# Five edits to a fused state-space, linear-attention and expert kernel: squares summed in pairs on VectorE, query decay spread by DMA, decay remainders on VectorE, step sizes two stages sooner, the second load of x into the first norm's buffer

## Time and profile before

| | us |
|---|---|
| median of 3 runs | 2577.02 (2574.51 to 2595.25) |
| the profiled execution | 2582.14, its span 2580.3 |
| opening of attention to opening of attention, one round | 1372.43 to 1495.92: 123.5 |
| PE busy in the span | 2221.5 (86%) |
| DVE busy | 1871.7 (73%) |
| ACT busy | 1469.4 (57%) |
| POOL busy | 813.6 (32%) |

### The profile page before, as it was taken

One profiled execution on the slowest core, in us unless ns is written; L12 is line 12 of the kernel. 1 busy time (PEld: TensorE's weight loads), 2 busy tenths in 40 slices (PEclk: granted clock), 3 DMA queues, 4 the chain that ended last, 5 costly groups with the idle time before them and its releaser, 6 DMA issues. The chain is left out here.

```text
span 2580.3 us, 53740 instructions
## 1 busy us (share of the span) xinstructions
PE 2221.5 (86%) x16824; PEld 1658.7 (64%) x16825; DVE 1871.7 (73%) x3521; ACT 1469.4 (57%) x3336; POOL 813.6 (32%) x1092
## 2 busy tenths in 40 slices
PE   3489898999889898989898989899989939999990
PEld 1247565666657565757575757575757739999990
DVE  2796869685968686777777786869685437777778
ACT  2276666665666566666666666667665603333334
POOL 0112414141414141414142323233242323334346
PEclk9599999998999899999999999999989969999995
DMA  4531414141423232323132223324140032222216
GB/s 121 119 90 43 103 38 99 41 97 40 97 58 84 53 83 68 79 61 87 51 87 66 71 66 71 86 52 98 39 107 5 10 132 58 59 57 56 60 46 195
DMA packets 144122, 189.19 MB, mean 73 GB/s; under 512 B 16984, under 2 KB 92768, under 8 KB 143552
## 3 DMA queue, kind: packets, MB, share of 16 engines
q1 hardware_dynamic: 121680, 118.72, 15.9%
q0 software_dynamic: 22272, 67.92, 12.4%
HBM read 109.77 MB, written 27.56 MB: 53 GB/s over the span
## 5 line engine op out<-in xcount | busy, mean ns | idle before, releaser
L1407 DVE TENSOR_TENSOR_SCAN hs<-decay,push 128x512 f32<-128x512 f32 x256 | 351.2, 1393 | 26.0 <-ACT decay L1069 20.5
L1156 ACT ACTIVATE S<-banks,fall_tok 128x128 f32<-128x128 f32 x1024 | 278.5, 385 | 28.4 <-PE banks L786 28.4
L978 PE MATMUL banks<-rowsT,w_here 128*128 128x128 f32 x2176 | 269.3, 277 | 7.3 <-DVE w_here L1731 7.3
L1512 DVE SCALAR_TENSOR_TENSOR oT<-tog,banks 128x512 f32<-128x512 f32 x128 | 87.6, 684 | 243.5 <-ACT sq L1123 243.3
L978 PEld LDWEIGHTS banks<-rowsT,w_here 128*128 128x128 f32 x2176 | 255.9, 193 | 10.7 <-issue 9.8
L1505 DVE TENSOR_TENSOR S<-banks,S 128x512 f32<-128x512 f32 x256 | 170.8, 687 | 104.2 <-PE banks L798 98.0
L1810 POOL DMA_DIRECT2D y<-ch x96 | 88.7, 924 | 498.8 <-DVE ch L1415 397.3
L1908 POOL TENSOR_TENSOR qd<-q,qd 128x512 f32<-128x512 f32 x96 | 134.1, 1397 | 292.0 <-ACT qd L1141 292.0
L1951 POOL DMA_INDIRECT results_scratch<-rows_out,result_to x136 | 132.3, 973 | 241.1 <-ACT rows_out L1285 234.4
L1274 ACT ACTIVATE tanh_h<-banks 128x512 f32<-128x512 f32 x136 | 81.3, 598 | 203.7 <-PE banks L978 203.7
L1069 ACT ACTIVATE decay<-delta,a_neg 128x512 f32<-128x512 f32 x256 | 171.9, 729 | 17.7 <-DVE hs L1407 17.1
(11 more groups left out here) (221 smaller groups left out, 5361.2 us busy)
## 6 DMA issues: line engine op xcount, KB each, us to landing
y<-ch POOLq DMA_DIRECT2D x96, 512.0 KB, 6.2
b_all<-bc_scratch SPq DMA_DIRECT2D x128, 256.0 KB, 5.5
c_all<-bc_scratch SPq DMA_DIRECT2D x128, 256.0 KB, 3.6
rows_in<-rows_scratch SPq DMA_DIRECT2D x136, 66.0 KB
both<-results_scratch SPq DMA_DIRECT2D x32, 256.0 KB, 3.5
w<-w_dram SPq DMA_DIRECT2D x3, 2048.0 KB, 8.9
x_tok<-x_dram SPq DMA_DIRECT2D x16, 256.0 KB, 3.3
x_again<-x_dram SPq DMA_DIRECT2D x16, 256.0 KB, 2.9
```

The costliest lines, as they stand in the source:

```text
L978: mm = pe.matmul(bank_h[:, u % 2, n, here], w_here[:, u % 2, n, here], x, start=True, stop=True)
L1156: ins = nc.scalar.activation(S[:, g, here], bank[:, here], ACT.Exp, bias=fall_tok[:, head:head + 1])
L1407: nc.vector.tensor_tensor_scan(hs[:, h, :], decay[:, n % 2, h, :], push[:, h, :], 0.0, ALU.mult, ALU.add).then_inc(s_scan, 1)
```

## The change

Five edits; both kernels compute the same function.

1. `sq_less`: DVE adds the two halves of `sq` (128x256) after each gating, and PE sums 4 blocks per chunk in place of 8. `project_out` waits for it.
2. The heads are stored even ones first. ACT takes exp(-fall) of 16 rows once per round into `fall_exp` (it shares the buffer of `sp_ln`), SP stores it to DRAM (two DMAs) and reads it back spread over 64 partitions each, twice per stage for stages 2 to 7, into `q_fall` with two slots. The uses `e`, their 24 matmuls per round and the 6 exponentials on ACT go; `chunk_fall` becomes a copy. POOL's multiplication reads `q_fall`. In a stage POOL now does `decay_queries` and the scatters ahead of `sum_state`. SP issues spreads 4 to 7 behind the last state's spread, each waiting for the multiplication two stages before it.
3. `fall_less` goes from POOL to DVE, in units 3 and 4.
4. `dt` goes to stage 4, DVE's part to stage 5; z goes to stage 6 and waits with its tanh for the step sizes.
5. The second load of x goes into `x1`, which is free only when the next sub-layer's sum is taken ("ffn", stage 6; before: "mix", stage 4). `take` copies to a buffer `x2_kept`, and the wait for the scatters moves to DVE's first `residual`, in stage 3.

```diff
 def front_uses(h):
 
     c, f = divmod(h, 2)
-    uses = [f"e{f}_{c}"] if c else []
-    uses += [f"v{f}_{c}"]
+    uses = [f"v{f}_{c}"]
...
-FRONT = {"xT": 0, "u0": 1, "u1": 2, "xdbl": 3, "z0": 5, "z1": 5, "dt0": 6, "dt1": 6}
-SIZES_STAGE, BC_STAGE, TAKE_STAGE, X3_AFTER = 7, 3, 2, 3
+FRONT = {"xT": 0, "u0": 1, "u1": 2, "xdbl": 3, "dt0": 4, "dt1": 4, "z0": 6, "z1": 6}
+SIZES_STAGE, BC_STAGE, TAKE_STAGE, X3_AFTER = 5, 3, 2, 4
+FALLS_AFTER = 3
+SPREAD_AFTER = {4: (2, 3), 7: (4, 5, 6, 7)}
...
             def body(i, j, n):
                 if i is not None:
                     if not first(i):
-                        drained(sp, ring, i - 1, "mix")
-                    sp.dma_start(x_again[:], x_dram[bass.ds(i, 1)].rearrange("b p c d -> (b p) c d")
+                        drained(sp, ring, i - 1, "ffn")
+                    sp.dma_start(x1[:], x_dram[bass.ds(i, 1)].rearrange("b p c d -> (b p) c d")
                                  ).then_inc(s_x_again, 16)
...
-                for m in range(STATES if i is not None else 0):
-                    spread_bc(m, i)
-                    if m == X3_AFTER and j is not None and not first(j):
-                        store_x3(j - 1)
-                if i is None and j is not None:
-                    store_x3(j - 1)
+                for m in range(STATES):
+                    if i is not None:
+                        spread_bc(m, i)
+                    if j is not None:
+                        if m == FALLS_AFTER:
+                            store_falls(j)
+                        if m == X3_AFTER and not first(j):
+                            store_x3(j - 1)
+                        for h in SPREAD_AFTER.get(m, ()):
+                            spread_falls(h, j)
...
+            def store_falls(j):
+
+                sp.wait_ge(s_fall_exp, at(j, 1, 1))
+                for odd in range(2):
+                    sp.dma_start(fall_dram[bass.ds(j, 1), odd].rearrange("b c h n -> (b h) c n"),
+                                 fall_exp[odd * PAIRS:(odd + 1) * PAIRS, :].rearrange("h (c n) -> h c n", n=P)
+                                 ).then_inc(s_fall_stored, 16)
+
+            def spread_falls(h, j):
+
+                c, f = divmod(h, 2)
+                if h == 2:
+                    sp.wait_ge(s_fall_stored, at(j, 32, 32))
+                if h >= 4:
+                    sp.wait_ge(s_qd, at(j, STAGES - 2, h - 3))
+                for odd in range(2):
+                    sp.dma_start(q_fall[odd * DH:(odd + 1) * DH, f, :],
+                                 fall_dram[bass.ds(j, 1), odd, c, 4 * f:4 * f + 4, :].rearrange(
+                                     "b h n -> b (h n)").broadcast_to([DH, 4 * P])).then_inc(s_q_fall[f], 16)
...
-                if c:
-                    bank, full = fill(ring, f"e{f}_{c}", j)
-                    for t in range(4):
-                        mm = pe.matmul(bank[:, t * P:(t + 1) * P], nselpair[:, 4 * f + t, :],
-                                       fall_parts[:, here], start=True, stop=True)
-                    mm.then_inc(full, 1)
...
                 pe.wait_ge(s_og, at(j, STAGES, 2 * c + 2))
+                pe.wait_ge(s_sq_less, at(j, STAGES, 2 * c + 2))
                 bank, full = fill(ring, f"wo_{c}", it)
                 for t in range(PAIRS):
                     pe.matmul(bank[:, 0:P], oT[:, t, :], w_o[:, t, :], start=(t == 0), stop=(t == PAIRS - 1))
-                for t in range(PAIRS):
-                    mm = pe.matmul(bank[:, P:P + 1], sq[:, t // 4, t % 4 * P:(t % 4 + 1) * P], ones[:, 0:1],
-                                   start=(t == 0), stop=(t == PAIRS - 1))
+                for t in range(PAIRS // 2):
+                    mm = pe.matmul(bank[:, P:P + 1], sq_less[:, t // 2, t % 2 * P:(t % 2 + 1) * P], ones[:, 0:1],
+                                   start=(t == 0), stop=(t == PAIRS // 2 - 1))
                 mm.then_inc(full, 1)
...
@@ -1041,7 +1066,7 @@
 
             def gate_input(h, n):
                 bank = full(ring, f"z{h}", n)
-                act.wait_ge(s_xc, at(n, HALVES, h + 1))
+                act.wait_ge(s_delta, at(n, HALVES, HALVES))
...
@@ -1053,7 +1078,8 @@
                 for h in range(HALVES):
                     nc.scalar.activation(delta[:, h, :], full(ring, f"dt{h}", n), ACT.Identity,
                                          bias=b_dt[:, h:h + 1]).then_inc(ring.free_sem(f"dt{h}"), 1)
-                drained(act, ring, n, "dt0", "dt1", "z0", "z1")
+                drained(act, ring, n, "dt0", "dt1")
+                act.wait_ge(s_xc, at(n, HALVES, HALVES))
                 nc.scalar.activation(th[:], delta[:], ACT.Abs).then_inc(s_sp, 1)
...
@@ -1093,6 +1120,7 @@
                 if n == 0:
                     act.wait_ge(s_fall, at(j, TILES, TILES))
                     nc.scalar.copy(fall_parts[:], fall[:]).then_inc(s_fsplit, 1)
+                    nc.scalar.activation(fall_exp[0:HEADS, :], fall[0:HEADS, :], ACT.Exp, scale=-1.0).then_inc(s_fall_exp, 1)
...
@@ -1134,11 +1163,10 @@
                 if h == 0:
                     after(act, s_O, at(j, STAGES, 0))
                 if c:
-                    falls = full(ring, f"e{f}_{c}", j).rearrange("p (t n) -> p t n", n=P)
+                    act.wait_ge(s_q_fall[f], at(j, 32 * (TILES - 1), 32 * c))
                     if c > 1:
                         act.wait_ge(s_decst, at(j, STAGES - 4, h - 3))
-                    nc.scalar.activation(chunk_fall[:, pairs], falls[:, :, P - 1], ACT.Exp).then_inc(s_kept, 1)
-                    nc.scalar.activation(qd[:, pairs, :], falls, ACT.Exp).then_inc(ring.free_sem(f"e{f}_{c}"), 1)
+                    nc.scalar.copy(chunk_fall[:, pairs], q_fall[:, f, P - 1::P]).then_inc(s_kept, 1)
...
@@ -1172,11 +1200,8 @@
             def take(j):
 
                 act.wait_ge(s_x2, at(j, TILES, TILES))
-                if not first(j):
-                    act.wait_ge(s_x3_stored, at(j, 16, 0))
-                    act.wait_ge(ring.full_sem("x3T"), ring.full_at("x3T", j))
-                    act.wait_ge(s_scattered, at(j, 16 * 2 * TILES, 0))
-                nc.scalar.copy(x3[:], x2_new[:]).then_inc(s_x2_taken, 1)
+                after(act, s_residual, at(j, TILES, 0))
+                nc.scalar.copy(x2_kept[:], x2_new[:]).then_inc(s_x2_taken, 1)
...
@@ -1199,11 +1224,11 @@
                             convolved(half, n)
                     if h == BC_STAGE:
                         parameters(n)
+                    if h == FRONT["dt1"]:
+                        steps(n)
                     for half in range(HALVES):
                         if h == FRONT[f"z{half}"]:
                             gate_input(half, n)
-                    if h == FRONT["dt1"]:
-                        steps(n)
...
+                after(dve, s_fall_exp, at(j, 1, 0))
...
+            def fall_less(n, j):
+
+                dve.wait_ge(s_fsplit, at(j, 5, 2 * n + 1))
+                if n == 0:
+                    nc.vector.tensor_tensor(fall_rest[:], fall[:], fall_parts[:], ALU.subtract).then_inc(s_fsplit, 1)
+                else:
+
+                    nc.vector.tensor_tensor(fall_rest[:], fall_rest[:], fall_parts[:], ALU.subtract).then_inc(s_fsplit, 1)
...
+                nc.vector.tensor_tensor(sq_less[:, f, :], sq[:, f, 0:2 * P], sq[:, f, 2 * P:4 * P], ALU.add
+                                        ).then_inc(s_sq_less, 1)
 
...
@@ -1587,11 +1628,11 @@
                     if h == NORM2_STAGE:
                         normalize(x2_new, s_rstd1, s_x2, i)
                 if n is not None:
+                    if h == SIZES_STAGE:
+                        step_sizes(n)
                     for half in range(HALVES):
                         if h == FRONT[f"z{half}"]:
                             gate_input(half, n)
-                    if h == SIZES_STAGE:
-                        step_sizes(n)
...
+                        if u in FALL_PARTS[:2]:
+                            fall_less(FALL_PARTS.index(u), j)
...
                 pairs = slice(4 * f, 4 * f + 4)
                 if c == 1:
                     drained(pool, ring, j, *(f"q{p}" for p in range(4 * f, 4 * f + 4)))
-                drained(pool, ring, j, f"e{f}_{c}")
-                nc.gpsimd.tensor_tensor(qd[:, pairs, :], q[:, pairs, c * P:(c + 1) * P], qd[:, pairs, :], ALU.mult
-                                        ).then_inc(s_qd, 1)
+                pool.wait_ge(s_q_fall[f], at(j, 32 * (TILES - 1), 32 * c))
+                pool.wait_ge(s_kept, at(j, STAGES - 2, h - 1))
+                after(pool, s_O, at(j, STAGES, h - 1))
+                nc.gpsimd.tensor_tensor(qd[:, pairs, :], q[:, pairs, c * P:(c + 1) * P],
+                                        q_fall[:, f, :].rearrange("p (t n) -> p t n", n=P), ALU.mult).then_inc(s_qd, 1)
...
             def stage(h, i, j):
                 m = STATE_IN_STAGE.get(h) if i is not None else None
-                if m is not None and m <= SUMS:
-                    sum_state(m, i)
```

(15 more changed lines are left out.)

38 lines of the change are left out of this document (16 added, 22 removed).

## The result

| | before | after |
|---|---|---|
| median, same chip | 2586.14 (2574.51 to 2611.83, 4 runs) | 2472.99 (2471.17 to 2474.75, 4 runs) |
| ratio, 95% interval | | 0.9576 (0.9539 to 0.9613) |
| span of the profiled run | 2580.3 | 2472.9 |
| granted clock over the span | 0.935 | 0.951 |
| opening to opening, mean of 12 rounds of the loop | 124.45 | 116.92 |

The kernel is 4.2% faster by the ratio. By these medians that is 113 us, and 104 against the 2577.0 from which the forecast started; forecast were 51. A round lost 7.5, not 3.1. (In this part a round is the mean of the same 12, worked out from PE's list: openings at 368.65 to 1862.09 before, 356.81 to 1759.82 after.)

A forecast was written before the change was run, and what follows sets the result against it. DVE was taken to set the pace from unit 2 to stage 2, PE from stage 3 on and in units 0 to 2. Terms summed to -3.1 per round, -51 together, giving 2526 from the median 2577.0; range 2490 to 2568.

The forecast's parts named there:

- 3.16 at the jump back of the loop: PE's wait at the loop's end, listed among the few places where PE stands still; no term was given for it.
- At the start of a round DVE is ready earlier, but its next work waits for the RMS scale, so nothing comes of it.: Start of a round: moving the step sizes earlier gains nothing there.
- Squares: PE's four one-column sums per round, halved: -0.85 for chunk 3 in unit 0, -2.55 for stages 2, 4 and 6.
- Pair products: PE's six sets of four matmuls dropped, stages 1 to 6: 0 in stages 1 and 2, -0.92 for the other four.
- Decay remainders: Moved from POOL to DVE beside the scans of states 2 and 3: -1.15 per round, bounds -2.6 to +1.4.
- Sum of squares on DVE: DVE's new additions, eight per round at 0.415; the first two, in DVE's regime, cost +0.8.
- Bank in stage 4: PE's second mask waits for DVE's state addition, delayed by collisions with POOL's products: +1.1 per round, 0 to 2.3.
- x1T copy: Stage 6: ACT copies the turned x1 behind its mask exponentials and PE waits: +0.5 per round, 0 to 1.5.
- Spreads, loads, scatters: The spreads' and next round's loads' DMAs stay covered, and the scatters have landed by DVE's stage 3: 0.
- slower rival: States' sum lands late and DVE stands 5.4 in stage 3: +2.3 per round, 2607; chance 0.07.
- faster rival: POOL's products miss DVE's new sums, so stage 4's wait is 0: -4.2 per round, 2509; chance 0.2.

The follow-up runs named there:

- e9: Changed kernel with 56 more PE instructions (satisfied waits) and the residual's load of x back in its own buffer behind stage 4's sum: 2507.09, ratio 0.9688.
- e7: Changed kernel with 56 more PE instructions per round, satisfied waits spread over places where PE stands anyway: 2536.53, ratio 0.9842 to the kernel before.
- e2: Changed kernel with edit 4 undone, so step sizes late again: 2508.37, ratio 0.9705 to the kernel before.
- e6: Kernel before with edit 4 alone, the earlier step sizes: 2580.48, ratio 1.000.
- e8: Changed kernel with edit 3 undone, POOL computing the decay remainders again: 2489.65, ratio 0.9651 to the kernel before.
- e3: Kernel before with edit 1 alone, squares halved on DVE and 4 sums per chunk on PE: 2549.04, ratio 0.984.
- e10: Changed kernel with DVE's halved sum of squares moved behind the state addition, in stage 7 behind x_new's normalisation: 2470.70, ratio 0.9546 to the kernel before.
- e11: Changed kernel with 24 more PE instructions per round, satisfied waits: 2473.61, ratio 0.9551 to the kernel before.
- e1: Changed kernel with 112 more PE instructions per round, satisfied waits ahead of two keys and the choice of experts: 2588.38, ratio 1.000 to the kernel before.

## Why the prediction was wrong, point by point

The direction was right, the size was half of what was measured. Compared by stretches of a round (predicted, measured): opening to x3's transpose -0.85, -2.12; from there to the scores of stage 3 -0.35, +0.72; the rest -1.87, -6.14.

- **The step that failed** is in the first paragraph: "3.16 at the jump back of the loop" was put down as a stall of fixed size and never priced. It was a fetch that hung on the length of PE's body. e9 is nearly the changed kernel with such a jump left in it (wait 2.78 by issue) and stands at 2507.1 where the changed kernel has 2471.5 on the same chip: the jump is worth some 35, or 2.8 a round, of which 1.6 are waiting and most of the rest the lower clock behind the opening.
- **The other terms were too small as well.** With the jump as it was, e9 is 81 faster than the kernel before on its chip (5.1 a round), where I had 51 (3.1). The terms below give some 1.6 of the missing 2.0: the bank in stage 4 and the copy of x1T that cost almost nothing, and the squares that gave more. The rest was not taken apart. e7 (2537) lies near my 2526 by luck: it has these gains and, by edit 5, a jump 1.7 longer than before.
- **"At the start of a round DVE is ready earlier, but its next work waits for the RMS scale, so nothing comes of it."** Wrong as soon as PE is not late itself: 2.5 a round (e2), in part the wait at x3, in part the clock at the end of the round. This and the fetch are no two separate terms.
- **Squares, -3.40:** from each start to the next work the one-column sums went from 7.10 to 3.25 a round, -3.85. Eight took 1.78 on average and four take 0.81, a little less than half; some 0.3 of it is the clock (e6, which has all eight: 6.82).
- **Pair products, -0.92:** the bf16 products of the shape of L816 in the earlier trace rows, masks and pairs together, went from 5.84 to 4.64, -1.20 for all six stages. That those of stages 1 and 2 turned into waiting fits the next waits, but no run has them alone.
- **Decay remainders, -1.15:** the size is confirmed by e8, 118.04 - 116.92 = 1.12; the price is clock more than waiting. And the 2.84 for one key became 1.62 and 1.47 for two, and behind the second and the choice's 1.27 PE fell to the lower clock (L849 at 1326.59 takes 2.87 for 1.89) in this round and two others of the 12.
- **Sum of squares on DVE, +0.8:** PE's waits for the state addition rose from 1.26 to 2.78 a round, this and the two pair products; e3, with the sums alone, has 1.72 between the scores of stages 0 and 3.
- **Bank in stage 4, +1.1 (0 to 2.3):** 0.15 in the changed kernel, 1.02 in e10. The collision is real; who starts first decides, and it fell on the cheap side, which I had not seen as a choice of its own. The 2.3 that I worked out by the Trainium skill's rule (SBUF — State Buffer, "SBUF: two separate sides"), with DVE paying both collisions in full, was too dear in both. By that rule the first to start gets the ports and the other is blocked; the traces agree, and the first was mostly DVE.
- **x1T copy, +0.5:** 0.75 for 0.68, so +0.07. ACT's last mask exponential ended at 1396.6, just as the transposes did.
- **Spreads, loads, scatters, 0:** no wait for `q_fall`, `b_all` 2.0 in all. The slower rival's place held as well: no wait of DVE for `y<-ch` in that round. What I missed is that the later loads would have queued ahead of an instruction fetch, 1.7 a jump in e7 against e9, had the body stayed long.

The faster rival assumed the same fixed jump; so did the lower end of my range. Its condition, a wait in stage 4 near 0, is the one that came true.

What stays open: the exact limit within 1713 to 1740 and what sets it; the first round of the pipeline, before the loop, which is 10 shorter (121.0 to 110.9; with edit 4 alone, e6, it is 115.7); what lowers the clock at the end of a round with late step sizes.

## What to carry to other kernels

A wait by issue at a loop's jump is not a constant: look at the instruction queues' packets, and if they grow with the rounds, count the instructions of the body; a few dozen may be worth more than the work they do (e7 to e11: 32 instructions, some 60 us). Where two late things arrive at the same place, removing one shows nothing, and edits tried one by one are then thrown away wrongly (e6: no gain alone, 35 us in company). Idle time is not the whole account either: here PE idled about as long after as before, and part of the gain was a higher granted clock. Loads that a change moves to the end of a loop stand ahead of the next fetch.

## What was not expected of the hardware

- Loop bodies of 1740 to 1806 instructions on PE are fetched again in each round, 9 blocks of 16.4 KB in most; at 1689, 1691 and 1713 they are not (e3, e6, e2, e11).
- The first packet after the jump begins when PE runs dry and PE works again 2.6 to 3.1 later (before, e9); with loads queued at that place, in one round 94% of the DMA engines' time, it began 0.4 to 3.4 later (e7).
- A satisfied wait on PE takes about 0.08 where many stand in a row (e1).
- A 128x512 product on POOL and a pair of them on DVE delay whichever starts second by about 1.0 to 1.1, in 23 of 24 rounds (e10, after); in e10 the first, POOL's, is 0.4 longer too.
